# Stationary pieces of 32 columns instead of 64 in three places of a two-layer gated cross-attention kernel

## The reference, cut to what matters

```python
# layer 0 attention (16 heads of 8); layer 1 is alike, with its values from per-head weights
q = Q @ Wq + bq ; k = K @ Wk + bk ; v = V @ Wv + bv
scores = jnp.einsum('bhqd,bhkd->bhqk', q, k) / jnp.sqrt(jnp.float32(D_K))
...
probs = jax.nn.softmax(scores, axis=-1)
out = jnp.einsum('bhqk,bhkd->bhqd', probs, v)
...
# layer 0 router, 8 logits a token
logits = jnp.einsum('bsd,ed->bse', x, router_w)
...
# layer 1 gates, 4 logits and 64 hidden values a token
h = jax.nn.relu(xf @ dp_w1 + dp_b1)
logits = xf @ gate_w + gate_b
```

## Time and profile before

| | |
|---|---|
| median of the runs | 1410.18 us (1409.01 to 1416.98, 3 runs) |
| span of the profiled execution, first to last instruction | 1173.7 us |
| attention of layer 0, first to last scores | 15.0 to 334.9 us, 32 steps |
| first mixture of experts | about 380 to 640 us |
| attention of layer 1, first to last scores | 656.8 to 939.1 us, 32 steps |
| second mixture of experts | from about 960 us |
| PE busy, share of the span | 1095.9 us, 93% |
| DVE busy | 902.1 us, 77% |
| ACT busy | 715.9 us, 61% |
| POOL busy | 543.8 us, 46% |

### The profile page before, as it was taken

One profiled execution on the slowest core, in us unless ns is written; L12 is line 12 of the kernel. 1 busy time (PEld: TensorE's weight loads), 2 busy tenths in 40 slices (PEclk: granted clock), 3 DMA queues, 4 the chain that ended last, 5 costly groups with the idle time before them and its releaser, 6 DMA issues.

```text
span 1173.7 us, 39887 instructions
## 1 busy us (share of the span) xinstructions
PE 1095.9 (93%) x13589; PEld 930.7 (79%) x13589; DVE 902.1 (77%) x3189; ACT 715.9 (61%) x1565; POOL 543.8 (46%) x699
## 2 busy tenths in 40 slices
PE   6899999999984899999999799999999979999998
PEld 4777777777762899999999577777777768999997
DVE  4778878889887454554543699999999979988886
ACT  4777778777760555555555577777777744444443
POOL 2112565556757334344443866666666421222230
PEclk7999999999996899999999899999999999999999
DMA  7223311111202333333333222222222100000000
GB/s 199 71 79 92 92 56 54 54 55 55 68 29 83 90 94 95 93 96 96 94 95 84 56 50 52 49 48 48 51 50 50 24 2 10 27 18 26 18 18 28
DMA packets 116781, 71.88 MB, mean 61 GB/s; under 512 B 51737, under 2 KB 105241, under 8 KB 116633
## 3 DMA queue, kind: packets, MB, share of 16 engines
q1 hardware_dynamic: 108440, 53.13, 16.8%
q0 software_dynamic: 8192, 16.79, 4.8%
HBM read 45.88 MB, written 22.94 MB: 59 GB/s over the span
## 4 chain that ended last, share of the span: by engine, by line
PE 69%; DVE 8%; ACT 7%; issue 7%; POOL 4%; SPq 2%; DMA 2%; DVEq 0%; ACTq 0%; POOLq 0%
PE ps_m L1741 11%; PE ps_m L1518 8%; PE ps_p L1506 7%; PE ps_s L1468 5%; PE ps_p L1622 5%; PE ps_m L1622 4%; PE ps_s L1478 4%; PE ps_s L1727 3%; PE ps_s L1728 3%; PE ps_s L1729 3%; ACT Kbd L749 3%; PE ps_m L1494 2%; ACT Pr L739 2%; PE ps_s L1610 2%; PE ps_s L1611 2%
## 5 line engine op out<-in xcount | busy, mean ns | idle before, releaser
L970 DVE TENSOR_REDUCE mx<-ps_s 128x8 f32<-128x512 f32 x256 | 168.7, 680 | 36.7 <-PE ps_s L1468 36.3
L1518 PEld LDWEIGHTS ps_m<-Vbd,PT 128*64 128x64 f32 x4096 | 137.8, 138 | 48.4 <-issue 42.8
L709 ACT ACTIVATE PT<-ps_p 128x512 f32<-128x512 f32 x256 | 152.7, 597 | 27.0 <-PE ps_p L1506 24.8
L1518 PE MATMUL ps_m<-Vbd,PT 128*64 128x18 f32 x4096 | 158.2, 213 | 0.2 <-ACT PT L709 0.2
L786 ACT ACTIVATE Kbd<-ps_s,c 128x512 f32<-128x512 f32 x128 | 87.3, 688 | 114.5 <-PE ps_s L1612 114.5
L1506 PE MATMUL ps_p<-cst,Pr 128*128 128x128 f32 x1024 | 155.2, 280 | 0.4 <-DVE orow L1246 0.4
L572 POOL TENSOR_TENSOR spare<-spare 1x1 f32<-1x1 f32 x99 | 21.1, 213 | 285.4 <-DVE b1s L1329 146.0
L648 POOL DMA_INDIRECT w1a<-louts,gi x128 | 125.5, 980 | 38.6 <-issue 29.5
L1741 PE MATMUL ps_m<-xn3T 128*128 128x128 f32 x1136 | 138.0, 275 | 0.2 <-ACT xn3T L851 0.2
L1741 PEld LDWEIGHTS ps_m<-xn3T 128*128 128x128 f32 x1136 | 132.7, 192 | 0.4 <-issue 0.4
L851 ACT ACTIVATE xn3T<-ps_s,b1s 128x256 f32<-128x256 f32 x284 | 111.2, 474 | 26.1 <-PE ps_s L1729 26.0
(11 more groups left out here) (219 smaller groups left out, 2695.8 us busy)
## 6 DMA issues: line engine op xcount, KB each, us to landing
xn3T<-lists SPq DMA_DIRECT2D x71, 128.0 KB, 2.1
louts<-xn3T SPq DMA_DIRECT2D x71, 128.0 KB, 1.9
ctxg<-in_ctxT SPq DMA_DIRECT2D x32, 256.0 KB
Kbd<-in_ctxT SPq DMA_DIRECT2D x512, 8.0 KB
out<-x SPq DMA_DIRECT2D x16, 256.0 KB, 2.3
w1a<-in_L_ffn_W SPq DMA_DIRECT2D x8, 256.0 KB, 3.3
w2a<-in_L_ffn_W SPq DMA_DIRECT2D x8, 256.0 KB, 4.0
Pr<-in_ctxT SPq DMA_DIRECT2D x16, 128.0 KB, 2.4
```

Of the source, the lines that this page charges most:

```text
L709: return nc.scalar.activation(dst, src, ACT.Copy)
L970: V.tensor_reduce(mx[g.par][:, q, :], per_key(ps_s[:, q, :]), AX, ALU.max).then_inc(max_done, 1)
L1518: ins = mm((bank7, bank6)[pr][S * b:S * b + S, VW * j:VW * (j + 1)], PT[c][:, P * i + S * b:P * i + S * b + S], Vbd[g.par][:, 2 * pr + b, ...
```

## The change

Three helpers of PE cut the stationary operand into pieces of 32 columns, where pieces of 64 stood. Four matmuls then write partitions 0 to 31, 32 to 63, 64 to 95 and 96 to 127, each in a column tile of its own, where two wrote halves. Operands, results, waits and signals are the same; the number of these matmuls doubles. The values of layer 1 (`late_values`, L1553) keep their pieces of 64.

```diff
@@ probs_by_values
-                    for b in range(2):
-                        ins = mm((bank7, bank6)[pr][S * b:S * b + S, VW * j:VW * (j + 1)],
-                                 PT[c][:, P * i + S * b:P * i + S * b + S], Vbd[g.par][:, 2 * pr + b, j, :],
+                    for r in range(4):
+                        ins = mm((bank7, bank6)[pr][32 * r:32 * r + 32, VW * j:VW * (j + 1)],
+                                 PT[c][:, P * i + 32 * r:P * i + 32 * r + 32], Vbd[g.par][:, 2 * pr + r // 2, j, :],
                                  start=True, stop=True)
@@ values
-                    for i in range(2):
-                        ins = mm(v_bank[S * i:S * i + S, S * b:S * b + S].rearrange("p (j d) -> p j d", j=8),
-                                 ctxg[g.par][:, b, 0, :], w[:, :, i, :], start=True, stop=True)
+                    for r in range(4):
+                        keys = slice(32 * (r % 2), 32 * (r % 2) + 32)
+                        ins = mm(v_bank[32 * r:32 * r + 32, S * b:S * b + S].rearrange("p (j d) -> p j d", j=8),
+                                 ctxg[g.par][:, b, 0, keys], w[:, :, r // 2, :], start=True, stop=True)
@@ logits
-                    for r in range(2):
-                        ins = mm(lg_bank[S * r:S * r + S, n * t:n * t + n], xn2T[g.par][:, P * t + S * r:P * t + S * r + S],
+                    for r in range(4):
+                        rows = slice(32 * r, 32 * r + 32)
+                        ins = mm(lg_bank[rows, n * t:n * t + n], xn2T[g.par][:, P * t + 32 * r:P * t + 32 * r + 32],
                                  w[:, :], start=True, stop=True)
```

## The result

The changed kernel takes 1434.94 us (median of 4 runs, 1432.9 to 1439.48), the kernel before 1413.58 us beside it. The ratio is 1.0166, 95% interval 1.0127 to 1.0205: 21 us slower, where 16 us less were forecast. The range given, 1385 to 1412, does not hold it. Executions of one kernel differ here (the kernel before took 1401 to 1446 us in 29 further runs), and a ratio leaves out those more than 1.5% above the fastest of their kernel, so 21 us are less than the spread of one kernel.

The account below looks back on a forecast made before the run. It took ACT's copies, with PE ahead of the first exponential, to bound layer 0, and PE, closely followed by DVE, layer 1. Savings of 6.5, 8.5 and 1.0 us took 1410.2 to 1394 us; range 1385 to 1412.

Parts of the forecast that it names:

- The base: Whole kernel: only the two attentions change; the rest of the 1173.7 us span and 236.5 us outside stay as they are.
- PE "full" in layer 1: Layer 1 attention: PE busy 239.84 of 240 us and alone in the chain, with DVE next at 231.4.
- a step that ends with `Vbd`: Layer 0 attention: scores wait for ACT's last copy into `Vbd` 24 times, 18.3 us in total.
- The pace of the small matmuls: Probabilities times values: a round falls from 58 to 32 ns, saving 0.83 us of PE a step.
- Values and logits: Values and layer 1 logits: no change, 58 ns a round; layer 0 logits fall 0.1 us a step in idle PE time.
- The sum: Both attentions: 6.5 + 8.5 + 1.0 us make 16.0 us saved, from 1410.2 to 1394 us.
- forecast 6.5: Layer 0: 24 steps that end with ACT each save 0.27 us, 6.5 us in all, bounds 3.6 and 9.4.
- forecast 8.5: Layer 1: DVE becomes the bound and regains its waits for PE, less 2 us for gathers: 8.5 us saved.
- forecast 1.0 for the ends: Last steps of both attentions, where the last group's product stands on the path: 1.0 us saved.
- The rivals: Three alternatives: four tiles load no faster (1410 us, 12%), records cost 29 ns each (1531, 9%), all PE savings count (1373, 4%).
- Slower, by a floor per record: Small matmuls in both attentions: each record costs some 29 ns whatever its width, 121 us slower, 1531 us; chance 9%.
- A drop of the granted clock as PE idles more: PE's clock in the profile after: a sign that the forecast is wrong, given no size or chance.

Follow-up runs that it names:

- new profile: Kernel before, unchanged, profiled again in one of its ordinary executions: 1427.05 us (10 runs), the profiled one 1407.28 us.
- direct kernel: All 256 indirect transfers of the attention steps replaced by direct ones of the same size: kernel before 1164.52 us, changed kernel 1148.85 us.
- version apart: Two of each four indirect transfers held until the step's third maximum, the others left at its end: kernel before 1305.78 us, changed kernel 1346.45 us.
- POOL's arithmetic: Kernel before with direct transfers, plus a POOL addition of 340 columns behind each of them: 1325.03 us.
- first profile: Kernel before, unchanged, the profile that the prediction read: span 1173.7 us, where its runs take 1410 us.

## Why the prediction was wrong, by its steps

**The base, wrong; this is the step that failed.** "... take the rest of the 1173.7 us span, and the 236.5 us outside of it, as they are." The difference between span and median was no constant part at the ends of the run, of which hardly 2 us are left in the new profile (1405.5 of 1407.28); it was time inside the attentions and between them that this one profiled execution had not lost. Of 231.8 us between the two profiles of the kernel before, 42.1 are in steps 8 to 24, 35.4 in steps 24 to 31, 32.7 between the attentions and 121.8 in layer 1 (table). PE "full" in layer 1 and a step that ends with `Vbd` describe that execution alone: in the ordinary one a step of layer 1 takes 13.4 to 13.7 us instead of 9.1, with PE's queue held up during POOL's indirect transfers. On that base the sum took 16 us off, and the change added 21; without indirect transfers it takes 15.7 off. 17% of the median were unexplained, and I set them aside in one sentence.

**The pace of the small matmuls, right.** 64 records in 0.74 us, loads of 112 ns without bursts (forecast 0.7 and 111). The floor per record, by which the rule of the Trainium skill in "TensorE: Matmul & The Clock Gate" would have made it 0.80 us a quarter, is not there across column tiles: a quarter takes 0.45 us with its last record.

**Values and logits, right in the steps without bursts and incomplete beside them.** 32 value records run 0.65 us in the direct kernel (185.80 us). Beside a burst they stand still instead: 24.7 us of `issue` waits of the loads in the ordinary changed kernel, in stretches like the one at 133.88 us.

**The sum, right on its own base, in part by luck.** From the two direct profiles: layer 0 saves 7.4 us (2.6 to step 8, 4.0 to step 24, 0.8 to step 31; forecast 6.5), layer 1 4.6 (forecast 8.5, bounds 5 and 12), behind the attentions 1.4 (forecast 1.0 for the ends), 12.9 in all; between the medians 15.7. So 15.7 beside 16 is closer than the terms are: layer 1's lies under its own lower bound in this pair. The profile of the changed kernel has one stretch more at the lower clock there, 6.8 us from 869 us on, which the windows show as 0.98 against 1.00 (changed and before, direct):

```profile
680.00:900.00 220.00, 214.20 (x5214) 152.27 (x5202) 215.48 (x814) 165.20 (x368) 107.82 (x195) 0.98 0.20 51
```

```profile
680.00:900.00 220.00, 220.00 (x3392) 166.41 (x3388) 212.04 (x797) 162.80 (x363) 107.47 (x195) 1.00 0.20 49
```

**The rivals.** None named a limit by place. "Slower, by a floor per record" had the sign and the unit, cost per record, but put it everywhere at 29 ns and came to 1531. The measured cost is 0.12 us a record in slow stretches and 0.012 elsewhere. "A drop of the granted clock as PE idles more" stood under what would be wrong, without a chance of its own. It came, 0.894 to 0.885, but behind the slow stretches and in the kernel before already.

**What the change loses to.** Shown: with no indirect transfers, or with half of them direct, the change gains 15.7 and 11.9 us; with two of four transfers beside its product it loses 41, and with the four laid one by one beside other work it gains 22. So the transfers turn the gain into a loss, and where they are laid decides how much. Not shown: how the 21 us in the original placement come about. Only 490 of the 7936 product records start during a burst there, fewer than the 1195 of the version that gains, so the number of pieces in the bursts does not account for them. In the ordinary profiles the changed kernel has 9.4 us more in layer 0 up to step 31, 25.1 more in layer 1 and 6.7 less between, and its steps of layer 1 vary from 11 to 19 us where those of the kernel before mostly take 13.4 to 13.7; but runs of one kernel differ by 40 us themselves. Open is also why one execution of the kernel before went through its bursts unharmed, and what an indirect transfer shares with PE's queue.

## What to carry to other kernels

Hold the profile's span against the median before reading anything else: if they differ by more than the few us at a run's ends (2 us here), the profile may be of an execution unlike the timed ones, and every wait in it is suspect until a second profile has been taken. A change that multiplies small instructions must be priced also at the slowest pace that its queue meets, not at the mean one alone. Where another engine's indirect transfers are in the way, look at them first: laying them elsewhere was worth over 100 us to either kernel here, and the change 16 at best.

## What the hardware showed that I had not expected

- During four or more indirect transfers of POOL in a row (0.95 to 1.03 us each, 0.3 apart) PE often starts only four to six records (loads with their matmul records) per 0.73 us, in the kernel before mostly from 2.1 us into the burst, in the changed one often from 0.6 us. Two in a row did little with the other two made direct (30 of 250 us), but held up the changed kernel's 32-column pieces in 73 of 90 bursts in the version apart. Direct transfers of the same bytes from the same engine show none of it. What they share with PE isn't in the trace. The Trainium skill, "SBUF — State Buffer", section "SBUF: two separate sides", sees contention at the port that GpSimd and Vector share and at the DMA's ports, and PE waiting for no one; the 850 ns of `xn` beside POOL's arithmetic agree with the first, the 3.20 us of the scores are not covered.
- The blocks in which PE's instructions are fetched are not it: 131 in the changed kernel with direct transfers as in the changed one with indirect ones. In the ordinary kernel before a block takes 1.0 us during a burst and elsewhere, and only 27 of its 91 fall into one, against 80 stretches. That agrees with the Trainium skill, "Runtime: NRT & Kernel Launch", section "Instruction fetch mechanics", where fetching ahead mostly hides behind execution.
- The granted clock fell to 0.50 behind slow stretches, as at 872.30 us, with PE's loads busy 0.94 of 3.50 us before; four transposes then take 1.06 us (872.60) where they take 0.60 at full clock (821.66 in the first profile), until the clock rises again after a window with PE busy 3.40 of 3.40 us. A second loss follows the first. The kernel before settles into a beat by it, steps of 13.4 to 13.7 us in layer 1; the changed kernel does not, its steps vary from 11 to 19.
